# PE's semaphore signals in a graph-attention kernel: two drains per group in place of increments on matmuls

## The reference, cut to what matters

```python
sent   = x[src] @ Ws + Ws_b
e_att  = sent + edges @ We + We_b
recv   = x[dst] @ Wr + Wr_b
logits = mish(e_att + recv) @ attn_w + attn_b        # per edge and head
w      = softmax of logits over the edges of one receiver
out    = layernorm(x + segment_sum(w * e_att, dst))
```

## Time and profile before

| | |
|---|---|
| median of 3 runs | 2175.18 us (2175.09 to 2179.09) |
| profiled execution, first to last instruction | 2661.8 us |
| mean granted TensorE clock in it | 0.835 of full |
| PE / DVE / ACT / POOL busy | 72% / 71% / 72% / 59% of the span |
| chain that ended last | DVE 36%, PE 20%, unknown queue 18%, issue 17%, ACT 7% |

### The profile page before, as it was taken

How to read it: one execution, slowest core, us unless ns; L and a number is a source line. 1 busy time by engine, 2 the same in 40 slices (tenths; PEclk the granted TensorE clock), 3 DMA queues, 4 the chain that set the end, 5 groups by cost and what they waited for, 6 DMA issues and landing times.

```text
span 2661.8 us, 45397 instructions
## 1 busy us (share of the span) xinstructions
PE 1917.4 (72%) x13621; PEld 1789.2 (67%) x13621; DVE 1895.0 (71%) x3941; ACT 1927.7 (72%) x3126; POOL 1575.1 (59%) x1640
## 2 busy tenths in 40 slices
PE   5667777777776777776776777776777777776776
PEld 5567666766666776766666766666667676666665
DVE  2676777777777767776676777766777777677766
ACT  1777777777777777777777777777777777777774
POOL 2666656656666665666566656656666666556661
PEclk8888888888888887888888888878888888878877
DMA  6422322322232322232232232232223232223220
GB/s 191 130 77 80 105 83 78 112 79 77 81 111 77 97 96 77 77 113 79 76 112 79 78 105 86 78 100 90 78 93 99 79 98 95 77 86 104 79 79 17
DMA packets 106714, 240.18 MB, mean 90 GB/s; under 512 B 45800, under 2 KB 72546, under 8 KB 99658
## 3 DMA queue, kind: packets, MB, share of 16 engines
q1 hardware_dynamic: 53334, 132.54, 14.6%
q0 software_dynamic: 52224, 107.06, 14.1%
q10 hardware_dynamic: 1128, 0.25, 0.0%
HBM read 229.98 MB, written 9.74 MB: 90 GB/s over the span
## 4 chain that ended last, share of the span: by engine, by line
DVE 36%; PE 20%; another core or an unknown queue 18%; issue 17%; ACT 7%; DVEq 1%; DMA 1%; ACTq 0%; SPq 0%
PE ps_sum L827 7%; DVE Z L1122 6%; DVE tbuf L1138 6%; DVE tbuf L1129 6%; DVE Z L1205 5%; PE ps_z L815 4%; PE ps_z L816 4%; DVE onehot L1113 4%; DVE logit L1144 2%; PE ps_edgeT L793 2%; ACT tbuf L933 1%; ACT tbuf L930 1%; ACT tbuf L936 1%; ACT tbuf L923 1%
## 5 line engine op out<-in xcount | busy, mean ns | idle before, releaser
L717 POOL DMA_INDIRECT landing<-xs_table,src_i x1632 | 1574.2, 965 | 1034.1 <-issue 448.3
L815 PE MATMUL ps_z<-we_sb,edgeT 128*128 128x128 f32 x3264 | 767.2, 320 | 83.3 <-issue 82.4
L816 PE MATMUL ps_z<-xr_buf,onehotT 128*128 128x128 f32 x3264 | 751.9, 315 | 72.3 <-issue 71.5
L827 PE MATMUL ps_sum<-Z,onehot 128*128 128x132 f32 x3264 | 558.9, 321 | 204.7 <-DVE att L1224 95.2
L815 PEld LDWEIGHTS ps_z<-we_sb,edgeT 128*128 128x128 f32 x3264 | 613.0, 232 | 100.9 <-issue 97.3
L816 PEld LDWEIGHTS ps_z<-xr_buf,onehotT 128*128 128x128 f32 x3264 | 609.4, 231 | 83.1 <-issue 82.8
L827 PEld LDWEIGHTS ps_sum<-Z,onehot 128*128 128x128 f32 x3264 | 485.6, 224 | 223.8 <-issue 149.4
L1113 DVE TENSOR_TENSOR onehot<-iota_f,ps_dve 128x512 f32<-128x512 f32 x408 | 276.0, 677 | 432.5 <-remote 352.6
L923 ACT ACTIVATE tbuf<-Z,c_zmax 128x512 f32<-128x512 f32 x408 | 296.2, 726 | 165.7 <-DVE Z L1122 85.9
L907 ACT COPY edgeT<-ps_edgeT 128x512 f32<-128x512 f32 x408 | 235.3, 577 | 229.4 <-remote 179.9
L798 PE MATMUL ps_onehotT<-ident_half,onehot 128*128 128x128 bf16 x1632 | 176.6, 232 | 241.8 <-issue 103.8
(11 more groups left out here) (110 smaller groups left out, 1228.3 us busy)
## 6 DMA issues: line engine op xcount, KB each, us to landing
landing<-in_edge_attr_dram SPq DMA_DIRECT2D x51, 2048.0 KB
landing<-xs_table,src_i POOLq DMA_INDIRECT x1632
x_in<-in_x_dram SPq DMA_DIRECT2D x51, 64.0 KB
xr_in<-xr_table SPq DMA_DIRECT2D x51, 64.0 KB
out_dram<-y_out SPq DMA_DIRECT2D x51, 64.0 KB
xr_buf<-xr_table SPq DMA_DIRECT2D x50, 64.0 KB
xs_table<-onehot SPq DMA_DIRECT2D x2, 896.0 KB
xr_table<-landing SPq DMA_DIRECT2D x1, 1568.0 KB
```

Of the source, the lines that this page charges most:

```text
L717: nc.gpsimd.indirect_dma_start(gath[b][:, t, :], None, xs_dram, bass.IndirectOffsetOnAxis(ap=src_i[:, b, t:t + 1], axis=0))\
L815: nc.tensor.matmul(ps_z[q][:, j, :], edgeT[:, q, j, :], we_sb[:, :], start=True, stop=False)
L816: mm = nc.tensor.matmul(ps_z[q][:, j, :], onehotT[:, q, j, :], xr_buf[:, b, :], start=False, stop=True)
L827: mm = nc.tensor.matmul(ps_sum[:, 0:ZC], OHv[:, b, t, :], Zv[:, b, t, :], start=(t == 0), stop=(t == T - 1))
```

## The change

Each signal of PE in a group was an increment carried by the last matmul of its set. Now `products` is followed by a drain of PE that carries the increment of `z_ps`. The two sets of transposes of `turn` are followed by one drain that carries `edgeT_ps`, and a semaphore instruction increments `onehotT_ps` behind it. `sums` signals nothing itself: `sum_ready` is incremented by a semaphore instruction in the next slot, behind the drain of that slot's products (`tell_sums`). Where a slot has no products (the last two windows), a drain of its own stands in.

```diff
 def turn(w, b, k, g):
     for j in range(n):
-        tr = nc.tensor.transpose(ps_edgeT[g % 2][:, j, :], edge_buf[:, b, a + j, :], ident[:, :])
-    tr.then_inc(edgeT_ps, 1)
+        nc.tensor.transpose(ps_edgeT[g % 2][:, j, :], edge_buf[:, b, a + j, :], ident[:, :])
     pe.wait_ge(onehot_ready, at(w, g))
     wait(pe, onehotT_ready, at(w, g) - 1)
     for j in range(n):
...
-    tr.then_inc(onehotT_ps, 1)
+    pe.drain().then_inc(edgeT_ps, 1)
+    pe.sem_inc(onehotT_ps, 1)

 def products(w, b, k, g):
...
-    mm.then_inc(z_ps, 1)
+    pe.drain().then_inc(z_ps, 1)

 def sums(w, b, g):
...
-    mm.then_inc(sum_ready, 1)

+def tell_sums(n):
+    if n:
+        pe.sem_inc(sum_ready, n)
+
 def window(w, b, k):
+    owed = len(SUM_NEXT[NG - 1]) if there(w - 2) else 0
     for g in range(NG):
         if there(w):
             products(w, b, k, g)
+        elif owed:
+            pe.drain()
+        tell_sums(owed)
+        owed = len(SUM_LAST.get(g, []) if there(w - 2) else []) + \
+            len(SUM_NEXT.get(g, []) if there(w - 1) else [])
```

More of the change, by code:

```diff
@@ L797, in turn @@
                 for j in range(n):
-                    tr = nc.tensor.transpose(ps_onehotT[:, j, :].bitcast(BF16)[:, 0:P],
-                                             halves(OHv[:, b, a + j, :]), ident_half[:, :])
-                tr.then_inc(onehotT_ps, 1)
+                    nc.tensor.transpose(ps_onehotT[:, j, :].bitcast(BF16)[:, 0:P],
+                                        halves(OHv[:, b, a + j, :]), ident_half[:, :])
+                pe.drain().then_inc(edgeT_ps, 1)
+                pe.sem_inc(onehotT_ps, 1)
             def products(w, b, k, g):
@@ L815, in products @@
                     nc.tensor.matmul(ps_z[q][:, j, :], edgeT[:, q, j, :], we_sb[:, :], start=True, stop=False)
-                    mm = nc.tensor.matmul(ps_z[q][:, j, :], onehotT[:, q, j, :], xr_buf[:, b, :],
-                                          start=False, stop=True)
-                mm.then_inc(z_ps, 1)
+                    nc.tensor.matmul(ps_z[q][:, j, :], onehotT[:, q, j, :], xr_buf[:, b, :],
+                                     start=False, stop=True)
+                pe.drain().then_inc(z_ps, 1)
             def sums(w, b, g):
@@ L826, in sums @@
                 for t in range(a, a + n):
-                    mm = nc.tensor.matmul(ps_sum[:, 0:ZC], OHv[:, b, t, :], Zv[:, b, t, :],
-                                          start=(t == 0), stop=(t == T - 1))
-                mm.then_inc(sum_ready, 1)
+                    nc.tensor.matmul(ps_sum[:, 0:ZC], OHv[:, b, t, :], Zv[:, b, t, :],
+                                     start=(t == 0), stop=(t == T - 1))
             def ends_to_row(w, b):
```

## The result

The changed kernel takes 2274.51 us (median of 6 runs, 2263.19 to 2278.80) beside 2175.14 us for the kernel before (6 runs): ratio 1.0449, interval 1.0425 to 1.0473. It is 99.4 us slower. One thing is needed to read the rows: the recording shown ahead of the prediction looks like those made where the kernel before itself takes about 2,600 us, and not the 2,175 us of its runs; experiment 1 shows such a place.

A forecast was written before the change was run, and what follows sets the result against it. Gathers were taken to pace the kernel at 39.9 us per window; the late signal lifts DVE from 38.0 to 42.3, carried as 42.55 us. 134.5 + 59.4 + 49 x 42.55 = 2279 us, range 2174 to 2385 us.

The forecast's parts named there:

- The pace before: POOL's 32 gathers, 1.25 us apart, pace the kernel before: 39.9 us of a 40.4 us window.
- 0.5 us without a name: Part of the 40.4 us window beyond the gathers' 39.9 us that the rows don't explain; half was carried.
- The recording's own: Recorded span of 2661.8 us against the 2175.18 us median: 486.6 us taken as caused by recording.
- The late `sum_ready` as the cost: The signal behind the next slot's products delays DVE in slots 5 to 7: 4.3 us more per window.
- The size of the stall: DVE's existing 1.39 us wait in slot 5, plus 3.5 us there, nothing in slot 6, 0.8 us in slot 7.
- the rival on the clock: PE holds 2.4 GHz in slot 5, so DVE stalls 2.3 us there: no change or 2182 us; chance 0.22.
- DVE takes over the pace: DVE's 38.0 us per window grows by 4.3 to 42.3 us, over the gathers' 39.9; 42.55 us carried.
- Drains at nothing where PE waits anyway: Two drains per group, 816 in all: 0.3 us each where PE is on the path, nothing where it waits.
- The cover: DVE runs 1.9 us per window behind the gathers (39.9 against 38.0), under which new DVE work can hide.
- the deferral does nothing: Rival: the runs have more cover, for instance slower gathers without a recorder, so 2175 us; chance 0.03.
- PE as the pace: Rival: drains keep PE longer at the low clock, 44.4 us per window, so 2370 us; chance 0.12.
- A gain from matmuls freed of increments: Rival: increments hold PE back in slots 5 to 7, at most 33 us, half giving 2160 us; chance 0.08.

The follow-up runs named there:

- experiment 1: The kernel before, recorded again without edit: 2611.11 us, beside 11 runs of it with a median of 2606.27 us.
- experiment 5: The kernel before, recorded without edit where its runs take about 2172 us: 2173.63 us.
- experiment 6: One gather in four left out: kernel before 2065.18 against 2174.24 us (slow place 2226.73 against 2606.27); changed kernel 2279.52 us, 1.0489 of the full kernel before.
- experiment 2: Changed kernel with sum_ready back on the sums' last matmul, both drains kept: 2178.84 us, 1.0027 of the kernel before; in the slow place 2840.04 against 2606.27 us.
- experiment 8: Changed kernel with sum_ready on a third drain right behind the sums: 2179.58 us against 2172.41 us for the kernel before, ratio 1.0029.
- experiment 3: Kernel before with only sum_ready late, on a drain behind the next slot's products: 2236.89 against 2172.41 us, ratio 1.0292; in the slow place 2691.21 against 2606.27 us.
- experiment 4: Kernel before with only the sum_ready of PE's slot 5 held back to a drain behind the next products: 2172.24 against 2174.27 us, ratio 0.9989.

## Why the prediction was right, point by point

- **The pace before.** The gathers set it, as forecast; experiments 5 and 6 show it. The window was 40.95 us and not 40.4 us: head and tail are 107.6 and 57.4 us elsewhere, not the 134.5 and 59.4 us of the slow recording. The forecast's 0.5 us without a name was 1.0 us, and the longer gathers of experiment 5, 1.28 us from one to the next on average and not 1.25 us, are that 1.0 us.
- **"The recording's own" 486.6 us.** Wrong. A recording takes as long as the runs, in both places (experiments 1 and 5). The stalls were left out of the sum, but it did take head, tail, the clock of slot 5 and the stall of 1.4 us from that recording. Head and tail cancel against the kernel before. The estimate of 2873 us for such a place was not put to the test.
- **The late `sum_ready` as the cost.** Right. Without it 0.3% is left (experiments 2 and 8), with it and its seven drains 2.9% (experiment 3).
- **The size of the stall.** 5.7 us per window were forecast (1.4 there already, 4.3 new); 5.5 us were measured (0.6 there already, 4.9 new). That the totals are so close is luck, because the parts were off in opposite directions. Slot 5: 4.9 us forecast, 3.27 us on average, and in no window more than 4.2 us. The sums themselves took 1.16 to 1.75 us there and never the 2.12 us of the earlier trace rows, and in 24 of 49 windows the products were at full clock too. So the rival on the clock had the stall of slot 5 right in half of the windows, 2.1 to 2.6 us against its 2.3 us, but not the time, for it took the same 0.8 us for slot 7. Slot 7: 0.8 us forecast, 1.90 us measured. In the window shown the missed term is ACT. When slot 5's one-hots are late, so is `add_gathered`, and ACT's activations start 2.7 us late, so its cast of the one-hots comes late and PE waits 0.81 us for the only `ps_onehotT` bank. The other missing part there is the drain behind the transposes, 0.36 us ahead of the sums. Experiment 3, which has no such drain, still waits 1.63 us in slot 7, so that drain is the smaller part; that ACT is the rest in every window is read from the one and not tested.
- **DVE takes over the pace.** 42.55 us per window forecast, 42.7 us measured, of which DVE is busy 1779.73 / 49 = 36.3 us and waits 5.5 us for the sums. Fewer gathers then change nothing (experiment 6).
- **Drains at nothing where PE waits anyway.** Right under cover (1.0027), at the 0.3 us each that the forecast took. Not small once the cover is gone: the part of the change that experiment 3 lacks, nine drains among it, brings 38 us. The forecast had priced drains within slots 6 and 7 and as 0.1 us in slot 5.
- **The cover.** 1.9 us per window were forecast, and it was more. Experiment 4 hides a stall that grew from 0.6 to 2.8 us, experiment 5 shows 2.9 us of waiting for gathers, and experiment 6 saves 2.2 us per window. New stall and cover were both forecast too small, and their difference came out: 2.1 us per window more forecast (42.55 less 40.4), 99.4 / 49 = 2.0 us measured. This is luck too. The rival "the deferral does nothing" was nearer than its chance of 0.03 said: it holds for slot 5 alone.
- **PE as the pace.** No. PE stands 2.21 us for `att` in the window shown, and its mean granted clock in the 49 windows rose to 0.97, from 0.93 in experiment 5. That rival's upper figure is also mis-added: 2370 us and half of 78 us make 2409 us, not 2385 us.
- **A gain from matmuls freed of increments.** None to be seen: experiments 2 and 8 are both slower than the kernel before. They add drains as they take increments away, and the gathers pace them, so a small gain of PE's own could not show.

## What to carry to other kernels

A signal is worth what stands between it and its reader: held back by one slot, it puts that slot's whole work into the reader's chain, though no arithmetic was added. Find the wait that the reader hides behind (here gathers, 2.9 us per window) and compare the sum of the new stalls with it, since one stall alone can vanish and two together not. For the same reason, don't add up the costs of parts that were measured one at a time. And check the recording's span against the runs first; where they differ by a fifth, get a second recording before calling it overhead.

## What the runs showed of the hardware

The kernel before takes 2166 to 2179 us in most sets of runs and 2596 to 2622 us in one, with the same instructions. Where it is slow, engines wait microseconds for PE's signals after the matmuls that carry them have ended by the record. An example from experiment 1: of PE's signals, these one-hots wait only for `sum_ready`, from sums that end at 144.79. DVE starts 9.1 us later, while PE itself has nothing to do from 148.56 on and waits for DVE:

```profile
143.59 1.20 PE L827 MATMUL ps_sum<-Z,onehot 128*128 128x132 f32 x8
...
147.96 0.60 PE L793 MATMUL ps_edgeT<-ident,landing 128*128 128x128 f32 x4
...
153.91 0.69 DVE L1113 TENSOR_TENSOR onehot<-iota_f,ps_dve 128x512 f32<-128x512 f32 x1 [7.66 <-remote]
...
154.66 0.61 PE L798 MATMUL ps_onehotT<-ident_half,onehot 128*128 128x128 bf16 x4 [6.09 <-DVE onehot L1113]
```

A drain waits there as well. In experiment 2 where it took 2840 us, the products end at 1009.32, and the work behind the drain starts 2.19 us later:

```profile
1008.93 0.39 PE L816 MATMUL ps_z<-xr_buf,onehotT 128*128 128x128 f32 x2
...
1011.51 0.65 PE L793 MATMUL ps_edgeT<-ident,landing 128*128 128x128 f32 x4 [2.19 <-issue]
```

Elsewhere the same kernel's longest wait there is 0.3 us. The word "remote" in the slow recordings names no second program: their traces hold 13,831 and 14,383 semaphore events, against 41,270 in experiment 5, so the event that would name the releaser is often missing.

Why PE's increments are late there is open, and so is whether it belongs to a chip or to a passing state. As the runs there have spans and granted clocks on record too, and not the recording alone, it is open as well whether the delay would be there if nothing were recorded. Whether a kernel with no increments on matmuls is spared is not known: neither the changed kernel nor the one with three drains was run there.
